# Delta rule, feed-forward, attention, feed-forward on one core: small products in two parts, roots from ScalarE alone, and three changes of order in the later stages

## The reference

```python
x = x + delta(layernorm(x))       # 8 heads of 128, two keys and values per token
x = x + ffn(layernorm(x))         # 256 -> 512 -> 512 -> 256, relu
x = x + attention(layernorm(x))   # 16 query heads on 4 key heads, causal
x = x + ffn(layernorm(x))
```

```python
state = state * exp(g_t)
for j in (0, 1):
    state = state + k_j x ((v_j - k_j state) * b_j)
o_t = q_t state;   o = o * rsqrt(mean(o * o) + 1e-5) * norm_w * silu(gate)
```

## Time and profile before

| what | value |
| --- | --- |
| median of three runs | 4109.01 us (4096.15 to 4117.0) |
| profiled execution | 4109.43 us, span 4107.6 us, mean granted clock 0.97 |
| TensorE busy over the span | 3812.3 us, 93% |
| VectorE, ScalarE, GpSimd | 68%, 54%, 38% |
| tables | 0 to 125.4 us, TensorE busy 70.1 |
| delta rule | 125.4 to 2247.1 us (2121.7), TensorE busy 2018.2 |
| feed-forward `f_` | 2247.1 to 2573.7 us (326.6), TensorE busy 282.6 |
| attention | 2573.7 to 3896.7 us (1323.0), TensorE busy 1252.8 |
| feed-forward `h_` | 3896.7 to 4107.6 us (210.9), TensorE busy 188.7 |

### The profile page before, as it was taken

One profiled execution on the slowest core, in us unless ns is written; L12 is line 12 of the kernel. 1 busy time (PEld: TensorE's weight loads), 2 busy tenths in 40 slices (PEclk: granted clock), 3 DMA queues, 4 the chain that ended last, 5 costly groups with the idle time before them and its releaser, 6 DMA issues. The chain is left out here.

```text
span 4107.6 us, 108406 instructions
## 1 busy us (share of the span) xinstructions
PE 3812.3 (93%) x38395; PEld 3174.9 (77%) x38395; DVE 2793.9 (68%) x7247; ACT 2233.8 (54%) x6182; POOL 1581.2 (38%) x2837
## 2 busy tenths in 40 slices
PE   6699999999999999999996899699999999999889
PEld 5588877788878888788885788577777877777678
DVE  5577777777777777777773544567777676676564
ACT  2466666666666666666662443344444444444354
POOL 0577677677776677677761000000000000000010
PEclk9999999999999999999996999899999999999999
DMA  4333333333333333333332321211111111110010
GB/s 171 116 87 87 109 94 101 86 91 110 94 97 87 98 109 87 107 94 104 86 98 73 126 75 37 89 44 42 56 40 51 39 56 35 56 56 29 28 62 31
DMA packets 543245, 322.36 MB, mean 78 GB/s; under 512 B 251744, under 2 KB 501088, under 8 KB 541024
## 3 DMA queue, kind: packets, MB, share of 16 engines
q1 hardware_dynamic: 542688, 315.21, 26.5%
HBM read 231.00 MB, written 84.01 MB: 77 GB/s over the span
## 5 line engine op out<-in xcount | busy, mean ns | idle before, releaser
L1038 DVE SCALAR_TENSOR_TENSOR g_conv<-g_r,g_taps,g_conv 128x511 f32<-128x511 f32 (+2 forms) x961 | 713.9, 743 | 28.2 <-issue 9.0
L2070 ACT ACTIVATE a_pr<-a_pr,a_low 128x128 f32<-128x128 f32 (+3 forms) x512 | 286.6, 560 | 391.3 <-DVE a_low L2215 374.5
L2370 POOL TENSOR_TENSOR a_dg<-a_const,a_fl 128x384 fp32r<-128x384 f32 x32 | 26.4, 827 | 1151.8 <-DVE a_fl L2222 1151.8
L2215 DVE CUSTOM_DVE_ANT_0 a_pr<-a_sc,a_bias 128x128 f32<-128x128 f32 (+3 forms) x512 | 242.2, 486 | 192.7 <-issue 172.8
L604 PE MATMUL g_r<-g_x_hi,g_w_hi 128*128 128x512 f32 x646 | 317.4, 491 | 10.0 <-issue 9.3
L901 ACT ACTIVATE g_us<-g_chn 128x128 f32<-128x128 f32 x528 | 146.4, 277 | 299.3 <-PE g_chn L710 296.1
L1898 PE MATMUL a_out<-a_pt,a_v 128*128 128x512 f32 (+3 forms) x1024 | 297.3, 433 | 0.9 <-DVE a_oT L2235 0.9
L1224 POOL TENSOR_TENSOR g_prod<-g_small 64x14 f32<-64x14 f32 (+6 forms) x896 | 227.3, 254 | 151.1 <-DMA g_small<-lower_d 85.8
L1226 POOL TENSOR_TENSOR g_small<-g_small,g_prod 64x14 f32<-64x14 f32 (+6 forms) x896 | 241.2, 269 | 70.3
L1066 DVE SCALAR_TENSOR_TENSOR g_R<-g_chn,g_ctab,g_bv 128x128 f32<-128x128 f32 x462 | 161.1, 349 | 154.4 <-PE g_chn L703 142.5
L1898 PEld LDWEIGHTS a_out<-a_pt,a_v 128*128 128x128 f32 x1024 | 184.7, 190 | 102.6 <-issue 62.2
(11 more groups left out here) (378 smaller groups left out, 11506.3 us busy)
## 6 DMA issues: line engine op xcount, KB each, us to landing
g_w_raw<-w_heads SPq DMA_DIRECT2D x66, 768.0 KB, 4.4
lower_d<-g_L SPq DMA_DIRECT2D x64, 512.0 KB, 3.6
g_U<-upp_d SPq DMA_DIRECT2D x64, 512.0 KB, 5.1
a_w<-w_groups SPq DMA_DIRECT2D x32, 640.0 KB, 4.5
oT_d<-g_oT SPq DMA_DIRECT2D x67, 256.0 KB, 5.0
g_T<-low_d SPq DMA_DIRECT2D x64, 256.0 KB, 3.0
g_T<-low_d SPq DMA_DIRECT2D x128, 128.0 KB, 3.4
f_oT<-oT_d SPq DMA_DIRECT2D x8, 2048.0 KB, 8.4
```

The lines of the kernel that those rows point to most:

```text
L1038: ins = V.scalar_tensor_tensor(out=y[:, k:L], in0=x[:, 0:L - k], scalar=tap, in1=y[:, k:L], op0=ALU.mult, op1=ALU.add)
L2070: A(pr[g % 2][:, i, 0:width(i)], pr[g % 2][:, i, 0:width(i)], ACT.Exp, scale=-1.0, bias=low[g % 2][:, i:i + 1], accum_out=tot[g % 2][:, i: ...
L2215: V.tensor_tensor_reduce(pr[g % 2][:, i, 0:width(i)], sc[i % 2][:, 0:width(i)], bias[tp_][:, i, 0:width(i)], -SCALE, 3.0e38, ALU.add, ALU. ...
```

## The change

Five edits. (1) `delta_rule`, TensorE: the 16 transposing products leave `un_small` for `turn_small`, which runs behind s5 (the three products of `chain_s`); `d_un` is still raised behind them. On VectorE the update of the state for chunk 5 goes ahead of all additions to `g_U`. (2) `delta_rule`: VectorE's `g_oden` goes, and ScalarE takes the root of each of the four columns by itself, with the division as its scale and the column of `g_qden` as its bias. (3) The `f_` stage alone: the transposes stand ahead of `layer_two(2)` and not `layer_two(3)`, the `columns` of ScalarE and VectorE ahead of `second(2)`, on VectorE also ahead of the last two `heads`. (4) Attention: the first scores go ahead of `value_rows` on TensorE, their exponentials ahead of its copies on ScalarE. (5) The clears between stages are dealt out to SyncE, ScalarE, VectorE and GpSimd in turn.

```diff
@@ delta_rule, TensorE: un_small is cut in two
                             M.matmul(lev[at_, c % 2, p, SM:2 * SM], T[h, c, at_], nu0[h, c, SM:2 * SM], start=True, stop=True)
+
+            def turn_small(u):
+
                 for p in range(HC):
...
                 if inverse:
                     un_small(u)
                 chain_s(u, q, 5, made)
+                if inverse:
+                    turn_small(u)
@@ ScalarE, end of a turn
                 ins.then_inc(s["d_osq"], 1)
-                act.wait_ge(s["d_oden"], u + 1)
-                A(osd[:], oden[:], ACT.Sqrt).then_inc(s["d_osd"], 1)
+                act.wait_ge(s["d_osq"], u + 1)
+                for m in range(TT):
+                    ins = A(osd[:, m:m + 1], oss[:, m:m + 1], ACT.Sqrt, scale=1.0 / P, bias=qden[(q + 2) % QN][:, m:m + 1])
+                ins.then_inc(s["d_osd"], 1)
@@ VectorE
+                chain_S(u, q, 5)
                 if inverse:
                     dve.wait_ge(s["d_un"], NLV * u + 1)
                     add_small(u, o, (1, 3))
-                chain_S(u, q, 5)
-                if inverse:
                     dve.wait_ge(s["d_Tc"], 2 * u + 1)
                     add_small(u, o, (0, 2)).then_inc(s["d_U"], 1)
...
-                dve.wait_ge(s["d_osq"], u + 1)
-                V.scalar_tensor_tensor(out=oden[:], in0=oss[:], scalar=1.0 / P, in1=qden[(q + 2) % QN][:], op0=ALU.mult, op1=ALU.add).then_inc(s["d_oden"], 1)
@@ feed_forward, TensorE
-                    if more and n == N2 - 1:
+                    if more and n == N2 - (2 if delta_out else 1):
                         turn_rows(b + 1)
@@ feed_forward, VectorE (ScalarE has columns(b + 1) ahead of second(b, 2) likewise)
                 second(1)
+                if more and delta_out:
+                    columns(b + 1)
                 if split:
                     heads(b + 2, (6, 7))
                 second(2)
-                if more:
+                if more and not delta_out:
                     columns(b + 1)
@@ attention, TensorE (ScalarE has exps(t + 1, 0, (0, 1)) ahead of value_rows likewise)
+                if nxt:
+                    scores(t + 1, 0, there, (0, 1))
                 if n >= 2 and more:
                     pe.wait_ge(s["xadd"], 2 * t)
                     value_rows(1 - bp, 0 if n == 2 else 3)
                 if nxt:
-                    scores(t + 1, 0, there, (0, 1))
@@ build
+                own = list(sems.values())
                 with nc.Block() as block:
                     @block.sync
                     def _(sp):
-                        for sem in sems.values():
+                        for sem in own[0::4]:
                             sp.sem_clear(sem)
+                    @block.scalar
+                    def _(act):
+                        for sem in own[1::4]:
+                            act.sem_clear(sem)
...
```

More of the change, by code:

```diff
@@ L444, in delta_rule @@
         osq = sb("g_osq", [P, TT, P])
-        oss, oden, osd, orec = (sb(f"g_{n}", [P, TT]) for n in ("oss", "oden", "osd", "orec"))
+        oss, osd, orec = (sb(f"g_{n}", [P, TT]) for n in ("oss", "osd", "orec"))
         on = sb("g_on", [P, TT, P])
@@ L1274 @@
           "d_kend", "d_qg", "d_nu", "d_nus", "d_un", "d_U", "d_Tc",
-          "d_ks", "d_R", "d_u", "d_us", "d_ds", "d_S", "d_o", "d_osq", "d_oden", "d_osd", "d_on", "d_ot", "d_oT", "d_dve"]
+          "d_ks", "d_R", "d_u", "d_us", "d_ds", "d_S", "d_o", "d_osq", "d_osd", "d_on", "d_ot", "d_oT", "d_dve"]
 def feed_forward(nc, io, sems, p, src, dst, delta_out):
@@ L2106, in turn @@
                     split_w(t + 2, here)
+                if nxt:
+                    exps(t + 1, 0, (0, 1))
                 if n >= 2 and more:
@@ L2109, in turn @@
                 if nxt:
-                    exps(t + 1, 0, (0, 1))
                     query(t + 1, 1)
@@ L2412, in _ @@
                     def _(sp):
-                        for sem in sems.values():
+                        for sem in own[0::4]:
                             sp.sem_clear(sem)
+                    @block.scalar
+                    def _(act):
+                        for sem in own[1::4]:
+                            act.sem_clear(sem)
+                    @block.vector
+                    def _(dve):
+                        for sem in own[2::4]:
+                            dve.sem_clear(sem)
+                    @block.gpsimd
+                    def _(pool):
+                        for sem in own[3::4]:
+                            pool.sem_clear(sem)
 def kernel(**inputs):
```

## The result

The changed kernel takes 4145.7 us (median of 6 runs, 4135.0 to 4156.1), the kernel before in the same comparison 4113.4 us (6 runs): a ratio of 1.0096, 95% interval 1.0072 to 1.0119. It is slower by 0.96%, where 0.2% was forecast. Six more runs of it on another occasion gave 4144.6 us against 4107.9, a ratio of 1.009 (1.0065 to 1.0115).

A forecast was written before the change was run, and what follows sets the result against it. TensorE, the busiest engine, was taken to bound the kernel. Delta rule +35 (19 + 22 + 12 - 18) and the rest -26.4 gave +8.6 on 4109.4, so 4118 us, range 4075 to 4146.

The forecast's parts named there:

- Clears: Ends of all four stages: dealing the semaphore clears out to four engines saves 7.9 us (6 to 9).
- first feed-forward: First feed-forward: earlier transposes shrink six waits for `f_xT_lo` from 1.7 to 0.2 us, -9 us (-10 to -7).
- Attention: Attention: scores ahead of `value_rows` cut the wait for `a_x` to 0.1 us in 14 turns, -9.5 us (-10.9 to 0).
- The split on TensorE: Delta rule: splitting the 48 small products around s5 adds changeovers, 0.30 us a turn, +19 us (13 to 22).
- The split on ScalarE: Delta rule: later small products delay ScalarE's chain, 0.5 us of wait at u6 and s6 in 37/53 turns, +22 us.
- The roots: Delta rule, turn's end: four roots add 0.4 us in 50 turns, less half the 15.6 us `g_on` waits, +12 us.
- The stalls: Delta rule: TensorE's 8.1 us of stalls ahead of L650 and four accompanying clock drops vanish, -18 us (-25 to 0).
- ScalarE's lateness everywhere: Rival, delta rule: s6 late in all turns, little roots relief, stalls move; 4153 us (4144 with half stalls' gain); chance 0.22.

## Why the prediction was wrong

At the same clock the sign of every part was right, and the time lies at the very edge of the stated range; but +8.6 was forecast and about +37 measured. By its own steps, at the same clock where not said otherwise:

**Clears and first feed-forward**: forecast -7.9 and -9. The four ends of stages are 6.8 us shorter in the profiles. `f_xT_lo` holds TensorE up only once now, at the first block, and of the 0.2 us expected at the transposes 0.1 at most appeared: the window is 7.3 us shorter besides its end. The runs give -12.5 ± 2.1 for both, 14 by the windows of these two traces. But the window of before is the shortest of its kind: over all thirteen traces it is 315.0 to 318.1 us with the edit and 326.6 to 330.6 without, 11.7 apart in the mean and 10.4 besides the end, which with the clears makes 17, as forecast. The clears were sized 1 too high; whether the feed-forward fell short, or some 4 us were lost again elsewhere, is open.

**Attention**: forecast -9.5. The wait went as said, and at the same clock it was worth 12. Measured it gave -7.5 alone, -6.6 on the other two, neither clear of noise (± 8), and nothing in the whole kernel (+6.7 ± 6.7, with 6 and 12 runs; there the clock is 0.0044 lower with it, 21 us by the line of the runs). On the mean of all runs some 6 us come back as a lower clock. The forecast had no term for that. It had the clock among what would make it wrong, but for the delta rule alone.

**The split on TensorE**: forecast 0.30 a turn, measured 0.30 to 0.33. Right.

**The split on ScalarE**: forecast 0.5 in a turn, and u6 and s6 as the places. Measured 0.17 and 0.13 of wait, with the slower starts behind them 0.5 (0.83 less 0.33). The size was right. The count was not: 37 of 53 turns were taken, 54 of 64 have it. Counted again, 45 of the 64 turns of before were tight, as the prediction has it, and nine more became so. Of these nine, four had a stall ahead of L650 that fell together with a low clock, four a stall ahead of L718 or L693, and one neither; with the split these stalls are gone, or shorter ahead of L730, and so is the slack. The stall ahead of L650 alone was no cover: eight other turns had it and were tight all the same. So the change itself took away the cover that this term relied on. 54 x 0.5 = +27 where +22 stood.

**The roots**: forecast +12, measured +14.9 ± 3.0. The two halves were both bigger and cancelled: 0.45 in all 64 turns (+29, forecast +20), and the whole 15.6 us of relief, not half. The estimate of 0.2 from one root to the next held (0.85 us for four). The Trainium skill ("ScalarE: Activation LUTs", What ACT_TABLE_LOAD costs) has 280 ns for an activation with a bias operand and 93 of overlap; the trace has 278 to 298 ns each and 0.19 between starts, so the page was right here, while its drain behind a table load is again not seen (2056.51 + 1.28, the exponential at 2057.80).

**The stalls**: forecast -18, of which 8.1 of standing still and some 10 of clock. The 8.1 went, and only these. The time at the lower clock in the delta stage did not fall: by the trace's record 150 us before, 137 to 164 in the other traces with the old order (one of 120), and 184, 164, 171, 157, 174 and 120 in the six with the split (records that begin in the stage; in each trace one of 72 to 89 us lies at its end, where it drains). I had read four turns in which a stall and a low clock came together, put the second down to the first, and took it that both would go. For these places that came true: none of the six traces with the split has a low stretch at L653 or L730, where before had four at L650 (13.6 us). But the low stretches that begin at the stalls ahead of L644, which stay, are longer: on average 3.8 us with the old order (53 of them in seven traces) and 6.2 with the split (55 in six), 57 us in a trace instead of 29. Why they are longer isn't shown. This is the step that failed most, by 10 us.

With 21 + 27 + 13 - 8 = +53 the delta rule comes out at what split and roots together measured, 52.7, against 35 forecast. The rest of the miss is the clock: the changed kernel ran at 0.9664, the kernel before at 0.9687, and 0.0023 are 11 us by the line of the runs. By the mean of all runs about half of that goes with the edit in attention, by the changed kernel with and without it all of it and more; what is chance in this (± 0.0012 on the 0.0023) and what another cause is not shown.

Of the rivals, ScalarE's lateness everywhere (4144 to 4153) came closest. Its point of decision was right: over two thirds of the turns, 54 of 64. Its time was met in part by luck: it says +35 to +44, and +26.3 was measured at the same clock, with 27 for its 31 at s6 and 15 for its 20 at the roots; 11 us of clock, for which it had no term either, made up the difference. It had been given 0.22 because some turns had slack.

## What to carry to other kernels

A stretch in which the chain is tight by a tenth of a microsecond cannot take another step ahead of the last small product: here ScalarE's table load came 1.00 us later (2.83 us behind the first small product instead of 1.83), 54 of 64 turns waited for it, an undisturbed turn paid 0.83, and the cost of a second such edit added up with it to the hundredth. When slack is counted turn by turn, ask whether the same change removes what made the slack. A gain in clock that is read from a few disturbed turns is no term of a sum: the low stretches that lay there went, and those at other stalls grew. An order that only takes rests from TensorE should be valued by its runs: here the best kernel keeps the delta rule as it was and takes the three later edits (mean 4089.6 us over 24 runs, -18.6; the ratios 0.9962 and 0.9951), and two thirds of its gain come from the feed-forward and the clears; the rest, 6.6 ± 7.7, isn't clear of noise.

## What the runs showed of the hardware

The time of a run follows its mean granted clock closely enough (4.76 us for 0.001, 4.5 us left over) to use the clock as a second measurement: it sharpens a difference of 12 us that the times alone leave open.

In the delta rule (to 2215 us, the one long stretch at its drain left out) the granted clock of these kernels falls to half only next to a wait of TensorE: of 192 such stretches in the thirteen traces 185 begin within 2 us of the end of a wait of 0.35 us or more, and all within 6. Not every such wait has one.

Standing still ahead of the small products goes with the instruction supply. In the trace of before, between 1200 and 1760 us, each of the seven such gaps at L644 and L650 ended 2.15 to 2.5 us after a 16 KB transfer of the instruction queue had begun, 1.2 to 1.6 us after it had landed; for all 22 between 300 and 2200 us it is 2.15 to 2.61 and 1.2 to 1.6. With three full products put between the two runs of small ones, the row of gaps ahead of the second is gone from the waits of every kernel with the split, and up to 0.5 us appeared three or four times ahead of L730. The Trainium skill ("Runtime: NRT & Kernel Launch", Instruction fetch mechanics) calls the crossing into the next block of instructions mostly hidden; here the gaps beside it are 0.4 to 1.2 us at small products, and 3.1 to 3.8 us at the head of the loop, where the page, too, warns of a taken branch. That small products use up the instructions faster than they come is argued from this; no run changed the supply itself.
